# A graph network in one kernel: each attention layer's division, residual, projection and next table inside the attention run

## What is computed

```python
def _gat_layer(h, W, al, ar, src, dst, residual):
    feat = (h @ W).reshape(N, H, D)
    el = jnp.sum(feat * al[None], axis=-1)
    er = jnp.sum(feat * ar[None], axis=-1)
    e = jax.nn.leaky_relu(el[src] + er[dst], NEG_SLOPE)
    m = jax.ops.segment_max(e, dst, num_segments=N)
    ex = jnp.exp(e - m[dst])
    den = jax.ops.segment_sum(ex, dst, num_segments=N)
    a = ex / jnp.maximum(den[dst], 1e-09)
    out = jax.ops.segment_sum(a[:, :, None] * feat[src], dst, num_segments=N)
    if residual:
        out = out + h.reshape(N, H, D)
    return jax.nn.relu(out).reshape(N, H * D)
```

## Time and profile before

| | us |
|---|---|
| median of 3 runs | 7459.04 |
| lowest and highest | 7442.75, 7459.76 |
| the profiled execution, its own time | 7455.44 |
| its span, first to last instruction | 7453.6 |

### The profile page before, as it was taken

One profiled execution on the slowest core, in us unless ns is written; L12 is line 12 of the kernel. 1 busy time (PEld: TensorE's weight loads), 2 busy tenths in 40 slices (PEclk: granted clock), 3 DMA queues, 4 the chain that ended last, 5 costly groups with the idle time before them and its releaser, 6 DMA issues. The chain is left out here.

```text
span 7453.6 us, 106044 instructions
## 1 busy us (share of the span) xinstructions
PE 5117.6 (69%) x16862; PEld 2947.9 (40%) x16862; DVE 4254.7 (57%) x11359; ACT 2953.5 (40%) x11888; POOL 4775.7 (64%) x5023
## 2 busy tenths in 40 slices
PE   2987777777777746667675666665666664667776
PEld 1444444443333323444443444433443433333333
DVE  3125555554444466767765677764677766444444
ACT  0320000000000047777775777774777774100000
POOL 0017777767777727777736777762777772577777
PEclk9997777777777777777776777787778777776666
DMA  3444444433333334444424444443444441333333
GB/s 107 149 143 118 118 118 118 117 101 105 106 106 106 106 117 132 137 134 134 135 82 120 134 134 134 137 113 122 134 134 134 137 134 48 98 112 112 112 111 106
DMA packets 481149, 885.83 MB, mean 119 GB/s; under 512 B 162507, under 2 KB 299637, under 8 KB 480694
## 3 DMA queue, kind: packets, MB, share of 16 engines
q0 software_dynamic: 240176, 662.04, 32.4%
q1 hardware_dynamic: 197264, 176.89, 7.2%
q10 hardware_dynamic: 43254, 41.93, 1.8%
HBM read 775.32 MB, written 102.58 MB: 118 GB/s over the span
## 5 line engine op out<-in xcount | busy, mean ns | idle before, releaser
L461 POOL DMA_INDIRECT rows_a<-table,stage_a x4992 | 4765.7, 955 | 2128.9 <-issue 1089.3
L586 PE MATMUL ps<-rows_a,hot_a 128*128 128x256 f32 (+1 forms) x4992 | 2130.8, 540 | 833.4 <-DMA rows_a<-table,stage_a 570.3
L1615 ACT ACTIVATE rows_a<-rows_a,ex_a 128x64 f32<-128x64 f32 x9984 | 2399.7, 334 | 0.0
L1671 PE MATMUL ps<-rows_a,hot_a 128*128 128x260 f32 x4992 | 1947.1, 512 | 263.0 <-DVE agg L1535 254.7
L549 DVE TENSOR_TENSOR agg<-agg,ps 128x256 f32 (+1 forms) x2496 | 1047.5, 420 | 1481.7 <-PE ps L586 1463.8
L586 PEld LDWEIGHTS ps<-rows_a,hot_a 128*128 128x128 f32 x4992 | 1077.5, 253 | 1800.1 <-DVE agg L549 905.3
L1671 PEld LDWEIGHTS ps<-rows_a,hot_a 128*128 128x128 f32 x4992 | 1019.9, 239 | 574.2 <-issue 439.3
L1535 DVE TENSOR_TENSOR agg<-agg,ps 128x260 f32 x2496 | 1037.6, 416 | 300.4 <-PE ps L1671 113.0
L1660 PE MATMUL ps<-am_a,hot_a 1*128 1x4 f32 x312 | 86.5, 345 | 553.7 <-DVE am_a L1518 553.7
L1804 ACT ACTIVATE root_a<-mv_a,eps 128x1 f32<-128x1 f32 x49 | 14.4, 295 | 1040.7 <-DVE mv_a L1827 1040.7
L1450 DVE TENSOR_TENSOR el_a<-rows_a,mneg 128x64 f32<-128x64 f32 x156 | 41.8, 268 | 651.3 <-DMA rows_a<-table,stage_a 651.3
(11 more groups left out here) (276 smaller groups left out, 3891.0 us busy)
## 6 DMA issues: line engine op xcount, KB each, us to landing
rows_a<-table,stage_a POOLq DMA_INDIRECT x4992, 2.8
dstt_a<-dloc_dram SPq DMA_DIRECT2D x156, 512.0 KB
table<-ob SPq DMA_DIRECT2D x50, 1024.0 KB, 4.4
table<-obg SPq DMA_DIRECT2D x149, 130.0 KB, 2.0
x_dram<-cur ACTq DMA_DIRECT2D x1, 6400.0 KB, 28.4
cur<-x_dram ACTq DMA_DIRECT2D x1, 6400.0 KB, 31.2
table<-ob SPq DMA_DIRECT2D x50, 128.0 KB, 1.7
table<-ob_a ACTq DMA_DIRECT2D x49, 128.0 KB
```

The source lines that it names most:

```text
L461: nc.gpsimd.indirect_dma_start(out=rows[:, j, 0:width], out_offset=None, in_=table, in_offset=bass.IndirectOffsetOnAxis(ap=stage[:, j:j + ...
L586: nc.tensor.matmul(ps[n % banks][:, 0:width], hot[:, m % nbuf, j, :], rows[:, n % RING, :], start=True, stop=True).then_inc(step_done, 1)
L1615: ins = nc.scalar.mul(a, a, ex[:, k % GV, s, h:h + 1])
L1671: nc.tensor.matmul(ps[j % banks][:, 0:W4], hot[:, j, :], rows[:, k % GV * UG + j, :], start=True, stop=True).then_inc(step_done, 1)
```

## The change

**Moved into the run.** `aggregate_gat` takes a helper class, `BesideGat` for the first two attentions and `BesideLast` for the third, and calls it at fixed places: on DVE before the addition of each step, on PE before each step's product, on ACT after each step's multiplications, on SP after the loads of each batch. `BATCH_OF` names the block that has had its last step before batch k (49 of the 52 batches have one). In that batch, for `BesideGat`: DVE takes the maximum (place 3), the reciprocal (4), the division (5) and the residual (7), PE turns the block (9) and multiplies it by the next weights (13), ACT makes a ReLU copy behind its last step and copies the product out in the next batch (place 7), SP stores it five batches later. The product of the weights with al and ar (`weigh`) stands in batch 1. For `BesideLast` the row statistics follow (places 8 and 11), the square root is taken for four blocks at a time on ACT (place 3), its reciprocal on DVE (0), and the block four before is normalised (1), turned (4) and multiplied (12). The last block, or the last five in the third run, follow behind the run's last step.

**Removed:** `weight_sums`, `gat_table`, `combine` and `row_stats`, the `project` of L3, the packing of block numbers, and the 50th block in these.

**Other edits:** the splitting of er stands at the start of the run on DVE, behind the clearing of `whole`; the factor of four columns moves from `ps[6]` to the bank `ps[4]`, and for that PE turns `el` of batch n behind the first product of batch k and waits for `fac_read`; the freed bank `ps[6]` is `slot_bank`; `dst_t` has two buffers and its load waits for one more batch of DVE; SP's loop is written out.

```diff
+    slot_bank = ps[6]
+    BATCH_OF = {-(-done_by(i) // UG): i for i in range(NB)}
+    LAG = 4
+    OUTS = 4
...
+        class BesideGat:
...
+            def act_first(self, act):
+                m = n + 1
+                act.dma_start(self.w[:, :, 0:D], w_view(gat_w[m])).then_inc(self.loaded, 16)
+                for q, a in enumerate((gat_al[m], gat_ar[m])):
+                    act.dma_start(self.av[:, q, :], a.rearrange("h d -> (h d)").partition_broadcast(P)).then_inc(self.loaded, 16)
...
+            def dve(self, dve, k, at):
+                if k == 1 and at in (3, 4, 6, 8):
+                    self.weigh(dve, (3, 4, 6, 8).index(at))
+                i = BATCH_OF.get(k)
+                if i is None:
+                    return
+                by_head = agg[:, i, :].rearrange("p (h w) -> p h w", h=H)
+                if at == 3:
+                    dve.wait_ge(self.added, self.banks + done_by(i))
+                    if i:
+                        dve.wait_ge(self.weighed, i)
+                    nc.vector.tensor_scalar(self.rd[:], by_head[:, :, DH:DH + 1].rearrange("p h o -> p (h o)"), 1e-9, None,
+                                            ALU.max).then_inc(self.most, 1)
+                elif at == 4:
+                    dve.wait_ge(self.most, i + 1)
+                    nc.vector.reciprocal(self.rd[:], self.rd[:]).then_inc(self.inverse, 1)
+                elif at == 5:
+                    dve.wait_ge(self.inverse, i + 1)
+                    if i:
+                        dve.wait_ge(self.joined, i)
+                    nc.vector.tensor_tensor(heads(self.part[:]), by_head[:, :, 0:DH],
+                                            self.rd[:].unsqueeze(2).to_broadcast([P, H, DH]), ALU.mult).then_inc(self.weighed, 1)
+                elif at == 7:
+                    dve.wait_ge(self.weighed, i + 1)
+                    if n == 0:
+                        if i == 0:
+                            dve.wait_ge(self.moved, 16)
+                        nc.vector.tensor_tensor(cur[:, i, :], self.part[:], cur[:, i, :], ALU.add).then_inc(self.joined, 1)
+                    else:
+                        nc.vector.scalar_tensor_tensor(out=cur[:, i, :], in0=cur[:, i, :], scalar=0.0, in1=self.part[:],
+                                                       op0=ALU.max, op1=ALU.add).then_inc(self.joined, 1)
+
+            def turn(self, pe, i):
+                pe.wait_ge(self.joined, i + 1)
+                if i:
+                    pe.wait_ge(self.taken, i)
+                nc.tensor.transpose(slot_bank[:, 0:P], cur[:, i, 0:P], ident[:])
+                nc.tensor.transpose(slot_bank[:, P:2 * P], cur[:, i, P:D], ident[:]).then_inc(self.turned, 1)
...
+            def pe(self, pe, k, at):
+                i = BATCH_OF.get(k)
+                if i is None:
+                    return
+                if at == 9:
+                    self.turn(pe, i)
+                elif at == 13:
+                    self.times(pe, i)
+
+            def copy_xt(self, act, i):
+                act.wait_ge(self.turned, i + 1)
...
+                nc.scalar.activation(self.xt[:].rearrange("p h e -> p (h e)"), slot_bank[:, 0:2 * P],
+                                     ACT.Relu).then_inc(self.xt_ready, 1)
+
+            def copy_out(self, act, i):
...
+                act.wait_ge(self.mm_done, i + 1)
...
+                nc.scalar.copy(heads(self.ob[:, u, :])[:, :, 0:DH], heads(slot_bank[:, 0:D]))
+                nc.scalar.copy(heads(self.ob[:, u, :])[:, :, DH:DH + 1].rearrange("p h o -> p (h o)"), slot_bank[:, D:D + H])
+                nc.scalar.copy(er_all[:, i, :], slot_bank[:, D + H:D + 2 * H]).then_inc(self.taken, 1)
+
+            def act(self, act, k, at):
+
+                if at == 7 and BATCH_OF.get(k - 1) is not None:
+                    self.copy_out(act, BATCH_OF[k - 1])
+                elif at == UG and BATCH_OF.get(k) is not None:
+                    self.copy_xt(act, BATCH_OF[k])
+
...
+    class BesideLast:
...
+        def dve(self, dve, k, at):
+
+            before = BATCH_OF.get(k - 1)
+            if at == 0 and before is not None and before % LAG == LAG - 1:
+                self.invert(dve, before // LAG)
+            i = BATCH_OF.get(k)
+            if i is None:
+                return
+            by_head = agg[:, i, :].rearrange("p (h w) -> p h w", h=H)
+            if at == 1 and i >= LAG:
+                self.normalise(dve, i - LAG)
...
+            elif at == 7:
+                if i == 0:
+                    dve.wait_ge(self.moved, 16)
+                dve.wait_ge(self.weighed, i + 1)
+                nc.vector.scalar_tensor_tensor(out=cur[:, i, :], in0=self.part[:], scalar=0.0, in1=cur[:, i, :],
+                                               op0=ALU.max, op1=ALU.add).then_inc(self.joined, 1)
+            elif at == 8:
+                dve.wait_ge(self.joined, i + 1)
+                if i:
+                    dve.wait_ge(self.spread, i)
+                nc.vector.bn_stats(self.st6[:], cur[:, i, :]).then_inc(self.stats, 1)
+            elif at == 11:
+                dve.wait_ge(self.stats, i + 1)
+                nc.vector.bn_aggr(self.mv[:, i, :], self.st6[:]).then_inc(self.spread, 1)
+
+        def roots(self, act, g):
+            of = self.group(g)
+            act.wait_ge(self.spread, of.stop)
+            nc.scalar.activation(self.root[:, of], self.mv[:, of, 1:2].rearrange("p b o -> p (b o)"), ACT.Sqrt,
+                                 bias=eps[:]).then_inc(self.rooted, 1)
...
+        def pe(self, pe, k, at):
+            i = BATCH_OF.get(k)
+            if i is None or i < LAG:
+                return
+            j = i - LAG
+            if at == 4:
+                if j:
+                    pe.wait_ge(self.taken, j)
+                self.turn(pe, j, slot_bank)
+            elif at == 12:
+                self.times(pe, j, slot_bank)
+
+        def act(self, act, k, at):
+
+            i, before = BATCH_OF.get(k), BATCH_OF.get(k - 1)
+            if at == 3 and before is not None and before % LAG == LAG - 1:
+                self.roots(act, before // LAG)
+            elif at == 7 and before is not None and before >= LAG:
+                self.copy_out(act, before - LAG, slot_bank)
+            elif at == UG and i is not None and i >= LAG:
+                self.copy_xt(act, i - LAG, slot_bank)
+
...
+        rest = tuple(range(NB - 1 - LAG, NB))
+
+        def dve_last(self, dve):
+            full, last = (NB - 1) // LAG - 1, (NB - 1) // LAG
+            self.invert(dve, full)
+            for q, at in zip(self.rest, ((3, 4), (5,), (7, 8), (11,))):
+                self.normalise(dve, q)
+                for a in at:
+                    self.dve(dve, KG, a)
+            self.invert(dve, last)
+            self.normalise(dve, NB - 1)
+
...
+    def aggregate_gat(name, table, beside, of_kind):
...
-        dst_t = sb(f"dstt_{name}", [P, GV, UG * P], BF, c)
+        dst_t = sb(f"dstt_{name}", [P, 2, UG * P], BF, c)
...
-        er_bank, fac_bank = ps[5], ps[6][:, 0:H]
+        er_bank, fac_bank = ps[5], turned[:, 384:384 + H]
...
+                    if k >= 2:
+                        sp.wait_ge(hott_ready, k - 1)
+                    if i:
                         sp.wait_ge(scans_done, k - (GV - 1))
...
+                behind = GV + 2
+                for k in range(KG + behind + 1):
+                    if k < KG:
+                        batch(k)
+                    after.sp(sp, k - behind)
+                after.sp_last(sp)
 
+                nc.vector.memset(whole[:], -BIG).then_inc(borders, 1)
+                part = lambda q: er3[:, :, :, q:q + 1].rearrange("p b h o -> p b (h o)")
+                nc.vector.tensor_copy(part(0), er_all[:]).then_inc(er_parts, 1)
                 nc.vector.tensor_copy(count, iota_f[:]).then_inc(counted, 1)
...
+                    after.dve(dve, k, j)
...
+                        after.act(act, k, s)
+                    after.act(act, k, UG)
+                after.act_last(act)
...
+                    if k:
+                        pe.wait_ge(fac_read, k)
...
+                        after.pe(pe, k, j)
...
                     n = k + 1 if k + 1 < KG else None
+                    sums(k, 0, 1)
                     if n:
                         turn(n)
-                    sums(k, 0, 1)
-                    if n:
                         er_of_edges(n, 0, er_rows(n, 0))
...
-        for n in range(3):
-            c = ExitStack()
-            if n:
-                weight_sums(n)
-                gat_table(c, n, gat_fill, 1, tables[1 + n], relu)
...
+        w = gat_weights(c, 0)
+        gam, bet = layer1_end(c)
+        first_gat_table(c, gam, bet, w)
         c.close()
         clear_sems()
+        x2 = x2_dram.rearrange("(b p) d -> p b d", p=P)
+        for n in range(3):
+            aggregate_gat(f"a{2 + n}", tables[1 + n], ((x2, cur[:]), None, (cur[:], x2))[n],
+                          BesideLast if n == 2 else next_attention(n))
```

(5 more changed lines are left out.)

348 lines of the change are left out of this document (189 added, 159 removed).

## The result

The changed kernel takes 7177.17 us, the median of four executions (7150.41 to 7179.32), against 7459.4 for the kernel before: a ratio of 0.9618, 95% interval 0.9592 to 0.9645. It is faster by 3.8%. The forecast was 7151 with a range of 7128 to 7192. The median lies in the range, 26 us above the forecast; the profiled execution, against whose predecessor the sum was made, took 7150.41 (span 7148.6), the lowest of the four. On the chip of the first experiments the same kernel took 7158.7 and the kernel before 7446.1, a gain of 287.4 us.

The account below looks back on a forecast made before the run. POOL's gather issue was taken to set the pace, with gaps between runs to be had. Gains 87.8 + 89.5 + 136.3 + 1.5 less 7.4 and 3.0 gave 304.7 us; 7455.4 less that is 7150.7, forecast 7151, range 7128 to 7192.

Parts of the forecast that it names:

- The gaps: Between runs: 103.7, 105.4 and 154.9 us shrink to 15.9, 15.9 and 18.6, gaining 87.8, 89.5 and 136.3 us.
- The tails: At the ends of the three attentions: no gather wait remains, so added work costs 2.0, 2.0 and 3.4 us.
- the slower rival: ACT's copy of the turned block, behind 64 multiplications, holds ACT; slower than before, some 7530 us at 7 us lateness; chance 0.02.
- The moved turn of `el`: On PE, behind one product: costs 0 to 0.3 us, within DVE's reserve.
- The moved work in mid-run: DVE gets 1.2 us per block in the first two attentions, 2.9 in the third, hidden in its gather waits.
- below 1 but not gone: Sign in the third attention: DVE's wait for gathers falls from 3.3 us to below 1 us but remains.
- the first rival: DVE sets the pace in the third attention, short by 0.8 to 0.9 us in 45 batches: 7191 us; chance 0.13.
- Contention: DVE's moved operations against POOL's gathers: 1 us per attention run, 3 in all.
- the second rival: Added DVE work stops POOL's gathers for its own length, 63 us over the attentions: 7211 us; chance 0.05.
- The rule of the shared port: A two-port VectorE copy, cast or tensor-scalar blocks GpSimd's descriptor writing for its whole length; time at most 7211 us.
- The table loads: ACT's third-attention loads, 1.28 us each, fit idle time; a rival at twice that costs 0 to 23 us, no chance given.
- The start: At the first attention's start, a 0.9 us barrier and the packing of block numbers go: 1.5 us gained.

Follow-up runs that it names:

- the first experiments: The changed kernel unedited and three edited versions of it, run on one chip; there the unedited one took 7158.68 us, the kernel before 7446.1 us.
- e8: The kernel before, unedited, profiled on the chip of two further runs: 7446.18 us, ratio 1.0000.
- e0: The changed kernel again, unedited, on another chip: 7158.68 us, ratio 0.9612 to the kernel before.
- e1: The changed kernel with PE's product of the moved block behind the last step in each attention's last batch: 7144.08 us, ratio 0.9596.
- e9: The kernel before with only the turn of el behind the first product and the factor columns in the turned rows' bank: 7462.40 us, ratio 1.0022.
- e11: The changed kernel with product behind last step, edge one-hot ahead of clearing, el's turn put back, factor columns in the er bank: 7135.87 us, ratio 0.9585.
- e4: The changed kernel with four more DVE tensor-scalars per batch with a block in the first two attentions: 7161.18 us, ratio 0.9623.
- e5: The changed kernel with four more DVE tensor-tensor additions per batch with a block in the first two attentions: 7169.39 us, ratio 0.9633.
- e2: The changed kernel with the first batch's edge one-hot ahead of the clearing of the sums in each attention: 7133.97 us, ratio 0.9582.
- e6: The changed kernel with the third attention's square root replaced by a copy, so no table loads there: 7153.50 us, ratio 0.9610.

## Why the prediction was right, and where not

The sum was 304.7 us; the profiled spans differ by 7453.6 - 7148.6 = 305.0. That the two agree is luck in the terms and in the executions. By the medians the gain is 282.2 us, and of later profiles e8 and e0 differ by 285.6: the three gaps give 326.6 us there, and the three attentions take back 40.0, where the prediction had 313.6 and 10.4. The terms, by the first two profiles:

- **The gaps**: forecast 15.9, 15.9 and 18.6, measured 13.5, 13.3 and 14.7 (12.5, 12.6 and 13.5 in e0). The mechanism was right, the gain 322.5 instead of 313.6 us. Too high were the way over the store and the barrier (4.35 + 0.93 forecast, 3.1 measured: both were read from the old stages, each with a wait of its own) and PE's five blocks (11 forecast, 8.5 to the last product's end, since PE turned the first of them early). From the division to the first copy out it was 4.3 against 4.0.
- **The tails**: forecast +2.0, +2.0 and +3.4, measured +5.5, +3.4 and +4.2. The step that failed is "the reserve is gone ... the added work counts in full": it counted durations and not PE's order. e1 shows 3.5, 3.3 and 1.5 us for the product that waits for ACT, e9 about 1 us for the turn. With both out of the way (e11) the tails are only 0.2, 0.6 and 2.2 us longer than in e8, so the added durations (2.0, 2.0 and 3.4) do not count in full either. The prediction had weighed exactly this copy behind 64 multiplications, but only as what holds ACT (the slower rival), not for what PE has behind it in the last batch.
- **The moved turn of `el`**: "0 to 0.3 us in DVE's reserve" was wrong. It is 0.87 us a batch of DVE's wait and, through gathers and tails, 17 us in all. It was the only small edit with a price: two buffers cost nothing, as forecast.
- **The moved work in mid-run**: forecast 1.2 us a batch in the first two attentions and 2.9 in the third. Measured from DVE's wait, with the 0.87 of the turn taken off: about 0.4 in the second (3.9 to 2.6) and 0.6 in the third (3.9 to 2.4). The operations fill pauses in which DVE waits for PE between additions (93.1 us of such waits in the second attention of e9, 65.5 in the changed kernel); the prediction had them each add their length. So DVE's pace was never near to being the bound, "below 1 but not gone" missed, and the first rival was further off than its 0.13.
- **Contention**: 1 us a run was forecast. Between the first two profiles the gathers without the blocked one grew by 3, 4 and 10 us (4, 5 and 17 from e8 to e0). In the first two attentions that is no more than the turn's share: e9 and e0 have the same sums, 794.9 and 796.5 against 795.0 and 796.8. In the third the moved operations add 8 to 13 us more. So 17 us (26) of the 63 of the second rival came, a good part of them by the turn; since the first gathers now stand earlier against the clearing, 13 us of them lengthen the way from the clearing to the last gather. The prediction priced the moved operations by their form. Their place against the gathers counts as well, and so does where they push DVE's other operations (last section).
- **The rule of the shared port**: a tensor-scalar was to hold POOL for its length. For the 384 more of e4 the trace shows 4 us in all, for the tensor-tensors of e5, for which the Trainium skill (SBUF — State Buffer, Who interferes with whom) expects no blocking of descriptor writing, 14. Neither is the price of the operations themselves. Gathers are held by tensor-scalars, but by two-input operations too (residual, division, second scan), and for the part of a gather that is left over, 0.1 us where it was most frequent, not for the operation's length. So the rule holds here in kind and not in price, and the two-input operations do what it says only of the others. At the start of a run a gather is held from before the tensor-scalar begins until it has run (e2).
- **The table loads**: inside their rows. The 0.75 to 1.54 us that ACT still waits with two loads in the batch exclude a switch of twice its row, and e6 excludes most of the rival's 23 us. The Trainium skill's drain of 1.38 us beside each load (ScalarE: Activation LUTs, What ACT_TABLE_LOAD costs) is not seen: the root starts 1.29 us after its load does, and no idle time stands before either load.
- **The start**: 1.5 us was forecast, the first clearing came 7.5 us earlier. 6.6 of these are there before the last copy of the stage ahead, which the change does not touch; the profiles of one kernel differ there by 3.6 us (changed kernel) and 4.0 (before).
- **Its own signs**: it would be wrong "if a run's length between the first and last gather changes by more than a few microseconds". It grew by 6.2, 2.9 and 12.0 us, so by that sign the prediction failed in the third run; and the mean gather there is 0.967 us even without the held one, above the 0.96 that was to show the second rival.
- **Slips in its figures**: the bounds of the three chains add -4 and +5 us, not -5 and +12; and 48 of a run's 52 batches have a block, not 49, since the last block follows the run.

So the errors were +9 (gaps), -6 (tails), -10 (mid-run), and +7 where executions scatter.

## What to carry to other kernels

When work moves into a loop paced by another engine, price it at the loop's end, not only in its middle. There each moved instruction counts by what is queued behind it in order, and one that waits for the end of another engine's batch must come behind the last of the loop's own. Look at the start too: the long clearing was harmless here, but what stood behind it held the engine that sets the pace. And since a pacing engine has no reserve, two per cent on its instructions (0.952 to 0.972 us on the mean, third attention, e8 to e0) cost 17 us, more than is left of a gap: compare their mean before and after any reordering, and find out which of the other engine's operations the longer ones end behind.
